# Lambda-layer block, float32, one core: all sixteen output tiles finished by VectorE in two passes

## The chip, the cores and the metric

The kernel runs on one core of a Trainium2 chip. The metric is the time of one execution on the device, in microseconds (us). The time before is the median of three runs.

## The reference: what is computed

The input x has 32 images of 512 channels and 64 x 64 pixels, float32. Per image, cut to what matters:

```python
xn = group_norm(x, 32 groups)                     # mean and variance over 16 channels x 4096 pixels
h = relu(bn1(conv1x1(xn, conv1_w)))               # 512 -> 128 channels
q = bn(conv1x1(h, q_w)); k = softmax(conv1x1(h, k_w)); v = bn(conv1x1(h, v_w))
pos = conv 15x15 of each of the 32 planes of v with 16 filters emb
out = einsum(q, k v^T) + einsum(q, pos)           # content and position parts, 4 heads x 32 = 128 channels
h = relu(bn2(out))
h = bn3(conv1x1(h, conv3_w))                      # 128 -> 512 channels
return x + relu(h + xn)                           # xn is the residual
```

The last line is what the change touches. With r the reciprocal deviation of the group (`rcur`), and b the folded bias less r times the group mean (`bcur`), it is x + relu(conv + r x + b), which equals max(conv + (1 + r) x + b, x).

## The kernel before

One image is worked on after the other, in a loop of 31 passes with a prologue for image 0 and an end for image 31. The order of the work is written out by hand, for each engine apart, and semaphores tie the engines together. One pass has two stages.

The lambda stage (`lam`): TensorE alternates between making the position weights (`w1.0` to `w5.7`, line 510, into the PSUM buffers `ring0` and `ring1`, moved to SBUF by ScalarE or VectorE on line 701) and multiplying them with V (line 655, into `ring2` and `ring3`). The content part (line 609) and a remainder (line 619) stand at its start and middle. VectorE takes the group statistics of the next image there.

The mixed stage (`mixed`, in the order `MIX`): it joins the front of the next image to the output of the present one. The front has four chunks of 1024 pixels: `c0` to `c3` (conv1, line 529), `q0` to `q3` (line 536), `k0` to `k3` (line 541, keys and values), the small products `nb`, `cl`, `cp`. The output has sixteen tiles of 128 channels x 1024 pixels, `o0.0` to `o3.3`; tile `oJ.T` has the number n = 4J + T. The stage ends with the first weights of the next image, `w0.0` to `w0.7`, and the remainders `r0`, `r1` (line 519). The order is

```python
c0 nb c1 q0 k0 o0.0 o0.1 c2 q1 k1 o0.2 o0.3 c3 q2 k2 o1.0 o1.1 q3 k3 o1.2 o1.3 o2.0 o2.1 cl o2.2 cp o2.3
o3.0 w0.0 o3.1 w0.1 o3.2 w0.2 o3.3 w0.3 w0.4 w0.5 w0.6 w0.7 r0 r1
```

TensorE fills one of the four 128 x 1024 PSUM buffers for each name and, before it does, waits until what the buffer held has been taken out (`take`, with the table `moved`). For the end of the stage the buffers are: `cl` follows `o1.2` in one buffer, `o2.2` follows `o1.3`, `cp` follows `o2.0`, `o2.3` follows `o2.1`, `o3.0` follows `o2.3`, `w0.5` follows `w0.3`, `w0.7` follows `w0.5`. `w0.0` waits, too, for the last quarter of the split q, which goes from SBUF to a DRAM buffer and back in another layout (`store_q`, `load_q` on SyncE's queue).

An output tile is finished in one of two ways. For a tile in `VEC_TILES` VectorE makes two passes: line 1022 adds (1 + r) x to the PSUM buffer in place, line 1025 adds the bias, takes the maximum with x and writes into X. For a tile in `POOL_TILES` VectorE makes one pass (line 1018: r x plus the PSUM buffer into an SBUF tile T, which lies in S and is double-buffered), ScalarE applies bias and relu to T (line 740), and GpSimd adds T to X (line 1174). In the second way the PSUM buffer is free after the one VectorE pass (`half_sum`), in the first after both (`out_ready`).

Of the eight weights `w0.s`, VectorE moves `w0.1` and `w0.5`, ScalarE the others. GpSimd also makes the third part of the split q (line 1167, once per chunk) and zeroes borders (line 1160). SyncE issues all transfers in one written order; in it, the outputs 8 to 15 come last, after the loads of V.

Of the kernel before, what the change touches and what calls it, by code (L numbers as in the profile page):

```python
# [43 lines left out]
STATS_AT = {0: (0, 0, 0, 0, 0, 1, 1, 1), 1: (1, 1, 1, 2, 1, 1, 2, 1), 2: (1, 1, 1, 2, 1, 1, 2, 1), 3: (1, 1, 1, 1, 1, 2, 1, 1)}  # L44


VEC_TILES = [1, 4, 7, 10, 13, 15]
POOL_TILES = [n for n in range(16) if n not in VEC_TILES]
NVEC, NPOOL = len(VEC_TILES), len(POOL_TILES)
HEAD = 1  # L50
# [42 lines left out]
def lambda_block(nc, x, w1, bn1, wq, bnq, wk, wv, bnv, emb, bn2, w3, bn3, out):  # L93
# [25 lines left out]
    with ctx:  # L119
# [169 lines left out]
        def moved(name, im):  # L289
# [10 lines left out]
            if name[0] == "o":  # L300
                n = int(name[1]) * CT + int(name[3:])
                if n in POOL_TILES:
                    return [(half_sum, im * NPOOL + HEAD + POOL_TILES.index(n) + 1)]
                return [(out_ready, im * NVEC + HEAD + VEC_TILES.index(n) + 1)]
            if name in ("gm", "gv", "nb", "r0", "r1", "cl", "cp"):
# [33 lines left out]
        def _(sp):  # L339
# [49 lines left out]
            def store_out(b, n):  # L389
# [3 lines left out]
                else:  # L393
                    sp.wait_ge(out_ready, b * NVEC + HEAD + VEC_TILES.index(n) + 1)
                sp.dma_start(ov[b, :, t, j * CHUNK:(j + 1) * CHUNK], X[:, j, t, :]).then_inc(out_done[j], 16)
# [451 lines left out]
        def _(dve):  # L847
# [157 lines left out]
            def output(chain, name, at, b):  # L1005
# [14 lines left out]
                else:  # L1020
                    i = VEC_TILES.index(n)
                    nc.vector.scalar_tensor_tensor(src[:, :], X[:, j, t, :], r1cur[:, t:t + 1], src[:, :],  # L1022
# [210 lines left out]
```

## Time and profile before

| what | us |
|---|---|
| median of 3 runs | 5392.46 (5383.96 to 5400.19) |
| the profiled execution: its own time | 5397.76 |
| its span | 5396.0 |
| TensorE matmul busy | 4680.3 (87%) |
| VectorE busy | 2873.9 (53%) |
| ScalarE busy | 2431.7 (45%) |
| GpSimd busy | 1047.7 (19%) |
| mean granted clock of TensorE | 0.91 |

The busy shares are means over an image; one image takes some 165 us, so the stages have to be read one by one. The rows below are of one image in the middle, whose mixed stage begins at 2534.64 us, and of the end.

### The profile page before, as it was taken

The page shows a single profiled execution, that of the slowest core. Times are in us where ns is not written, and L with a number is a line of the kernel's source. Part 1 is how long each engine was busy: PE and PEld are TensorE (multiplying, and loading weights), DVE is VectorE, ACT ScalarE, POOL GpSimd, SP SyncE. Part 2 cuts the span into 40 slices and gives each one's busy share as a digit, 9 for nine tenths or more (in the row PEclk, how much of TensorE's full clock was granted, in tenths as well). Part 3 has the DMA queues.
Part 4 walks back from the last instruction along what each step waited for, and adds up shares of the span by engine and source line. Part 5 has one row for each costly group of instructions (what it writes and reads, how often), then busy time and mean ns, then how long its engine had stood idle before and what let it go on. Part 6 is the DMA issues. An engine that isn't in the chain of part 4 may idle for free.

```text
span 5396.0 us, 121678 instructions
## 1 busy us (share of the span) xinstructions
PE 4680.3 (87%) x49366; PEld 2721.4 (50%) x49366; DVE 2873.9 (53%) x4567; ACT 2431.7 (45%) x2944; POOL 1047.7 (19%) x561
## 2 busy tenths in 40 slices
PE   4888899888889888898888988889988899888897
PEld 2554455554455544555544555445554455554454
DVE  4455555555554555555555555555455555555553
ACT  1444445444444444444444444444444444444444
POOL 0012221122211122211222111222112221122222
PEclk8898899988998898998899998899998899998998
DMA  3668766678666677666786666876667766678666
GB/s 99 196 220 267 253 192 224 218 240 273 218 206 226 220 265 258 192 220 217 240 273 196 212 220 230 273 238 187 225 228 253 264 191 221 220 233 274 232 194 214
DMA packets 540245, 1217.09 MB, mean 226 GB/s; under 512 B 54313, under 2 KB 236589, under 8 KB 539821
## 3 DMA queue, kind: packets, MB, share of 16 engines
q1 hardware_dynamic: 539820, 1210.21, 67.8%
q8 instruction: 416, 6.82, 0.5%
q14 instruction: 9, 0.07, 0.0%
HBM read 777.68 MB, written 365.22 MB: 212 GB/s over the span
## 4 chain that ended last, share of the span: by engine, by line
PE 63%; SPq 11%; DMA 8%; issue 7%; DVE 6%; ACT 3%; POOL 1%; ACTq 0%; POOLq 0%; DVEq 0%
PE ring L529 16%; PE ring L510 15%; PE ring L655 12%; PE ring L585 7%; DMA q_parts<-region 6%; SPq L356 5%; PE ring L609 4%; PE ring L536 3%; PE ring L541 2%; SPq L363 2%; ACT region L701 2%; DMA Qt<-q_parts 2%; DVE region L701 2%; PE ring L619 2%; SPq L366 1%
## 5 line engine op out<-in xcount | busy, mean ns | idle before, releaser
L701 ACT COPY region<-ring 126x1024 f32<-126x1024 f32 x1184 | 1162.1, 1015 | 1324.4 <-PE ring L510 1307.0
L585 PE MATMUL ring<-h,w3T 128*128 128x512 f32 x2048 | 1047.9, 653 | 141.9 <-DVE S L1018 119.0
L510 PE MATMUL ring<-Qt,Ep 96*126 96x256 bf16 x5120 | 871.5, 309 | 341.2 <-issue 156.1
L1174 POOL TENSOR_TENSOR X<-X,S 128x1024 f32<-128x1024 f32 x320 | 750.7, 2351 | 1147.3 <-ACT S L740 1147.3
L510 PEld LDWEIGHTS ring<-Qt,Ep 96*126 96x126 bf16 x5120 | 622.3, 152 | 659.0 <-issue 483.6
L529 PE MATMUL ring<-X,w1e 128*128 128x512 f32 x2048 | 906.4, 595 | 28.8 <-DVE w1e L895 28.8
L701 DVE COPY region<-ring 126x1024 f32<-126x1024 f32 x352 | 430.8, 1224 | 915.3 <-PE ring L510 914.7
L655 PE MATMUL ring<-region,V 126*32 126x128 f32 x24576 | 857.4, 283 | 18.0 <-DVE region L701 9.9
L655 PEld LDWEIGHTS ring<-region,V 126*32 126x32 f32 x24576 | 654.6, 113 | 143.5 <-issue 117.9
L585 PEld LDWEIGHTS ring<-h,w3T 128*128 128x128 f32 x2048 | 396.9, 207 | 547.8 <-issue 365.1
L529 PEld LDWEIGHTS ring<-X,w1e 128*128 128x128 f32 x2048 | 384.5, 190 | 495.3 <-issue 492.0
L871 DVE BATCH_NORM_STATS2 st<-X 128x6 f32<-128x512 f32 x1024 | 624.2, 679 | 0.0
L740 ACT ACTIVATE S<-S,bcur 128x1024 f32<-128x1024 f32 x320 | 366.7, 1146 | 538.6 <-DVE S L1018 534.2
L973 DVE SCALAR_TENSOR_TENSOR region<-ring,pbi,region 64x512 f32<-64x512 f32 x256 | 179.4, 739 | 787.6 <-ACT region L790 566.8
L1018 DVE SCALAR_TENSOR_TENSOR S<-X,rcur,ring 128x1024 f32<-128x1024 f32 x320 | 405.6, 1275 | 121.7 <-PE ring L585 119.1
L1167 POOL TENSOR_TENSOR region<-region 64x1024 bf16<-64x1024 f32 x128 | 273.0, 2133 | 936.1 <-ACT region L794 931.2
L1160 POOL MEMSET region<- 64x224 f32 x32 | 13.2, 413 | 2259.1 <-PE ring L655 2215.2
L784 ACT ACTIVATE region<-ring,nb 128x1024 f32<-128x1024 f32 x128 | 142.0, 1109 | 506.4 <-DVE nb L902 299.4
L1022 DVE SCALAR_TENSOR_TENSOR ring<-X,r1cur,ring 128x1024 f32<-128x1024 f32 x192 | 246.7, 1285 | 206.8 <-PE ring L585 202.4
L541 PEld LDWEIGHTS ring<-wkvT,region 128*128 128x128 f32 x2048 | 238.2, 191 | 103.9 <-issue 77.9
L541 PE MATMUL ring<-wkvT,region 128*128 128x48 f32 x2048 | 254.1, 277 | 0.0
L609 PE MATMUL ring<-Qt,CLp 96*32 96x512 bf16 x1024 | 245.8, 1092 | 7.2 <-DMA Qt<-v_rest 7.2
(127 smaller groups left out, 3018.7 us busy)
## 6 DMA issues: line engine op xcount, KB each, us to landing
X<-x_dram SPq DMA_DIRECT2D x256, 2048.0 KB, 11.9
out_dram<-X SPq DMA_DIRECT2D x512, 512.0 KB, 6.6
Qt<-q_parts SPq DMA_DIRECT2D x768, 128.0 KB, 2.8
V<-v_windows SPq DMA_DIRECT2D x96, 1024.0 KB, 10.9
h<-S SPq DMA_DIRECT2D x1024, 64.0 KB, 2.0
q_parts<-region SPq DMA_DIRECT2D x128, 256.0 KB, 4.5
v_windows<-region SPq DMA_DIRECT2D x64, 512.0 KB, 6.1
V<-v_windows SPq DMA_DIRECT2D x32, 672.0 KB
```

What stands on the lines that cost most here:

```text
L510: last = nc.tensor.matmul(dst[0:TROWS, i * 256:(i + 1) * 256], taps(u, xo, yo), Q[:, :, xo * BLK + yo, :], start=(i % 2 == 0), stop=True, ...
L529: last = nc.tensor.matmul(dst[:, hh * HALF:(hh + 1) * HALF], w1e[:, c, :], X[:, j, c, hh * HALF:(hh + 1) * HALF], start=(c == 0), stop=(c ...
L541: last = nc.tensor.matmul(dst[:, i * KV:(i + 1) * KV], h1[:, j % 2, i * P:(i + 1) * P], wkvT[:, :], start=True, stop=True)
L585: last = nc.tensor.matmul(dst[:, yb * HALF:(yb + 1) * HALF], w3T[:, t, :], src, start=True, stop=True)
L609: nc.tensor.matmul(bank_of(k)[c * DV:(c + 1) * DV, :], CLp[:, :], Qg[:, :, c, half * 32:half * 32 + 32, 4 * k:4 * k + 4] .rearrange("p h n ...
L655: last = nc.tensor.matmul(bank_of(i)[c * DV:(c + 1) * DV, (g % 4) * P:(g % 4 + 1) * P], V[0:TROWS, VSLOT[t], xb, yb * DV:(yb + 1) * DV], W ...
L701: return engine_copy(dst, src)
L740: nc.scalar.activation(T[:, i % 2, :], T[:, i % 2, :], ACT.Relu, bias=bcur[:, n % CT:n % CT + 1]).then_inc(half_relu, 1)
L871: return nc.vector.bn_stats(st[:, c, 2 * j + hh, :], X[:, j, c, hh * HALF:(hh + 1) * HALF])
L1018: nc.vector.scalar_tensor_tensor(T[:, i % 2, :], X[:, j, t, :], rcur[:, t:t + 1], src[:, :], ALU.mult, ALU.add).then_inc(half_sum, 1)
L1167: nc.gpsimd.tensor_tensor(q12[:, 1, cols], r1[:, j % 2, :], q12[:, 0, cols], ALU.subtract)\
L1174: nc.gpsimd.tensor_tensor(X[:, j, t, :], X[:, j, t, :], T[:, i % 2, :], ALU.add).then_inc(pool_out, 1)
```

## The change

One line of the tables changes; all sixteen numbers stand in `VEC_TILES` now, and `POOL_TILES` is empty, so that `NVEC` is 16 and `NPOOL` is 0:

```diff
-VEC_TILES = [1, 4, 7, 10, 13, 15]
+VEC_TILES = list(range(16))
 POOL_TILES = [n for n in range(16) if n not in VEC_TILES]
 NVEC, NPOOL = len(VEC_TILES), len(POOL_TILES)
```

What this does to VectorE's instructions at two places follows. The first is the loop's part from `o1.2` to `o2.3` (tiles 6 to 11), with the small products `cl` (L994) and `cp` (L997 to L1003) between them. Before:

```order
L1018 SCALAR_TENSOR_TENSOR S<-X,rcur,ring 128x1024
L1022 SCALAR_TENSOR_TENSOR ring<-X,r1cur,ring 128x1024
L1025 SCALAR_TENSOR_TENSOR X<-ring,bcur,X 128x1024
L1018 SCALAR_TENSOR_TENSOR S<-X,rcur,ring 128x1024
L1018 SCALAR_TENSOR_TENSOR S<-X,rcur,ring 128x1024
L994 COPY Qt<-ring 16x32
L1022 SCALAR_TENSOR_TENSOR ring<-X,r1cur,ring 128x1024
L1025 SCALAR_TENSOR_TENSOR X<-ring,bcur,X 128x1024
...
L1003 CAST CLp<-clt 96x32
L1018 SCALAR_TENSOR_TENSOR S<-X,rcur,ring 128x1024
```

And now:

```order
L1022 SCALAR_TENSOR_TENSOR ring<-X,r1cur,ring 128x1024
L1025 SCALAR_TENSOR_TENSOR X<-ring,bcur,X 128x1024
L1022 SCALAR_TENSOR_TENSOR ring<-X,r1cur,ring 128x1024
L1025 SCALAR_TENSOR_TENSOR X<-ring,bcur,X 128x1024
L1022 SCALAR_TENSOR_TENSOR ring<-X,r1cur,ring 128x1024
L1025 SCALAR_TENSOR_TENSOR X<-ring,bcur,X 128x1024
L1022 SCALAR_TENSOR_TENSOR ring<-X,r1cur,ring 128x1024
L1025 SCALAR_TENSOR_TENSOR X<-ring,bcur,X 128x1024
L994 COPY Qt<-ring 16x32
L1022 SCALAR_TENSOR_TENSOR ring<-X,r1cur,ring 128x1024
...
```

Four tiles ahead of or at `o2.3` (`o1.2`, `o2.0`, `o2.1` and `o2.3` itself) have a second pass that was not there. The second place is the end of the mixed stage on VectorE, from the move of `w0.1` to that of `w0.5` (L701), with the tiles `o3.2` and `o3.3` between them:

```order
 L701 COPY region<-ring 126x256x4
 L1009 REGISTER_ALU
-L1015 REGISTER_ALU
-L1018 SCALAR_TENSOR_TENSOR S<-X,rcur,ring 128x1024
-L1022 SCALAR_TENSOR_TENSOR ring<-X,r1cur,ring 128x1024
-L1024 REGISTER_ALU
+L1022 SCALAR_TENSOR_TENSOR ring<-X,r1cur,ring 128x1024
+L1025 SCALAR_TENSOR_TENSOR X<-ring,bcur,X 128x1024
+L1022 SCALAR_TENSOR_TENSOR ring<-X,r1cur,ring 128x1024
 L1025 SCALAR_TENSOR_TENSOR X<-ring,bcur,X 128x1024
 L910 REGISTER_ALU
 L701 COPY region<-ring 126x256x4
```

The second pass of `o3.2` now stands ahead of the move of `w0.5`. On ScalarE and GpSimd the ten instructions of line 740 and the ten of line 1174 go from each image; GpSimd keeps the four of line 1167. SyncE's transfers and TensorE's matmuls keep their order; ten of the output stores wait for VectorE where they waited for GpSimd.

## Rows read from the trace of the kernel before

**Rows 1.** The page: chain that ended last, shares of the span.

```profile
PE 63%; SPq 11%; DMA 8%; issue 7%; DVE 6%; ACT 3%; POOL 1%; ACTq 0%; POOLq 0%; DVEq 0%
```

**Rows 2.** Windows of one image: busy us (instructions) of each engine, clock, DMA.

```profile
2595.79:2613.10 17.31, 11.47 (x78) 5.94 (x78) 12.78 (x18) 4.59 (x4) 9.36 (x4) 0.77 0.76 201
2613.10:2634.35 21.25, 16.16 (x57) 8.90 (x56) 11.18 (x10) 10.40 (x11) 4.70 (x2) 0.66 1.02 346
```

**Rows 3.** Waits of TensorE: us in total, times, longest us.

```profile
PE ring L585 <- DVE S L1018: 119.0, 31, 3.9
PE ring L510 <- DMA Qt<-q_parts: 108.6, 32, 7.6
```

**Rows 4.** Timeline of TensorE, `cl` to `o3.1`: start us, us, line, [idle before].

```profile
2597.88 3.13 PE L557 MATMUL ring<-region,kS 128*16 128x32 f32 x64 [2.09 <-DVE S L1018]
...
2609.32 3.78 PE L585 MATMUL ring<-h,w3T 128*128 128x512 f32 x4 [3.75 <-DVE S L1018]
2616.20 1.11 PE L510 MATMUL ring<-Qt,Ep 96*126 96x256 bf16 x4 [3.10 <-DMA Qt<-q_parts]
2617.10 3.62 PE L585 MATMUL ring<-h,w3T 128*128 128x512 f32 x4
```

**Rows 5.** TensorE's shortest `o3.0`, in another image.

```profile
4597.22 1.98 PE L585 MATMUL ring<-h,w3T 128*128 128x512 f32 x4 [3.89 <-DVE S L1018]
```

**Rows 6.** VectorE's groups by line: busy us, mean ns of one.

```profile
L1022 DVE SCALAR_TENSOR_TENSOR ring<-X,r1cur,ring 128x1024 f32<-128x1024 f32 x192 | 246.7, 1285 | 206.8 <-PE ring L585 202.4
L1025 DVE SCALAR_TENSOR_TENSOR X<-ring,bcur,X 128x1024 f32<-128x1024 f32 x192 | 246.6, 1284 | 6.8
```

**Rows 7.** Timeline of VectorE, `k3` to `o2.3`, the same image.

```profile
2592.21 1.38 DVE L986 TENSOR_TENSOR kS<-kS,kst 128x128 f32<-128x128 f32 x1
...
2594.06 1.81 DVE L959 TENSOR_TENSOR kS<-kS,kst 128x128 f32<-128x128 f32 x1
...
2596.55 1.28 DVE L1018 SCALAR_TENSOR_TENSOR S<-X,rcur,ring 128x1024 f32<-128x1024 f32 x1
...
2603.41 1.29 DVE L1022 SCALAR_TENSOR_TENSOR ring<-X,r1cur,ring 128x1024 f32<-128x1024 f32 x1 [0.36 <-PE ring L585]
...
2606.43 1.06 DVE L1000 CAST clh<-clt 96x32 bf16<-96x32 f32 x1
```

**Rows 8.** Timeline of GpSimd beside it.

```profile
2591.09 2.35 POOL L1174 TENSOR_TENSOR X<-X,S 128x1024 f32<-128x1024 f32 x1 [5.18 <-ACT S L740]
2593.60 2.12 POOL L1167 TENSOR_TENSOR region<-region 64x1024 bf16<-64x1024 f32 x1 [0.16 <-POOL X L1174]
...
2602.79 4.66 POOL L1174 TENSOR_TENSOR X<-X,S 128x1024 f32<-128x1024 f32 x2 [1.28 <-ACT S L740]
```

**Rows 9.** L1000 over all images: ns min/median/max.

```profile
L1000 DVE CAST clh<-clt x32: 178/1386/1401, 133.0 to 5252.3; 96x32 bf16<-96x32 f32 x32
```

**Rows 10.** Timeline of VectorE, `o3.1` to the move of `w0.5`.

```profile
2620.76 1.29 DVE L1022 SCALAR_TENSOR_TENSOR ring<-X,r1cur,ring 128x1024 f32<-128x1024 f32 x1 [6.25 <-PE ring L585]
...
2624.41 1.27 DVE L1018 SCALAR_TENSOR_TENSOR S<-X,rcur,ring 128x1024 f32<-128x1024 f32 x1
2625.95 1.29 DVE L1022 SCALAR_TENSOR_TENSOR ring<-X,r1cur,ring 128x1024 f32<-128x1024 f32 x1 [0.26 <-PE ring L585]
...
2628.51 1.23 DVE L701 COPY region<-ring 126x1024 f32<-126x1024 f32 x1
```

**Rows 11.** Timeline of the end on VectorE: the first passes and the last.

```profile
5360.34 1.28 DVE L1018 SCALAR_TENSOR_TENSOR S<-X,rcur,ring 128x1024 f32<-128x1024 f32 x1 [16.35 <-PE ring L585]
5362.06 1.29 DVE L1022 SCALAR_TENSOR_TENSOR ring<-X,r1cur,ring 128x1024 f32<-128x1024 f32 x1 [0.43 <-PE ring L585]
...
5364.58 2.46 DVE L1018 SCALAR_TENSOR_TENSOR S<-X,rcur,ring 128x1024 f32<-128x1024 f32 x2
...
5389.18 1.28 DVE L1025 SCALAR_TENSOR_TENSOR X<-ring,bcur,X 128x1024 f32<-128x1024 f32 x1
```

**Rows 12.** Timeline of the end, GpSimd's last.

```profile
5389.20 2.34 POOL L1174 TENSOR_TENSOR X<-X,S 128x1024 f32<-128x1024 f32 x1 [1.23 <-ACT S L740]
```

## Prediction

> **What bounds the kernel now.** I read the chain that ended last first. TensorE holds 63% of it, and VectorE only 6% [rows 1], so VectorE's added work counts only where TensorE waits for it. The waits of TensorE say where that is: 119.0 us in 31 waits of an output tile for a VectorE pass of line 1018, and 108.6 us in 32 waits of a weight for the split q to come back from DRAM [rows 3]. The timeline of one image puts both in the last third of the mixed stage [rows 4]: `cl` waits 2.09 us for the pass of `o1.2`; `o3.0` waits 3.75 us, at 2609.32, for the pass of `o2.3`, which held its PSUM buffer; and `w0.0`, two rows on, waits 3.10 us, at 2616.20, for q. The windows agree: between 2595.79 and 2613.10 VectorE is busy 12.78 of 17.31 us and TensorE 11.47, at a mean granted clock of 0.77, and in the next 21.25 us the clock is 0.66 [rows 2]. Of the ten tiles that get a second pass, those before `o1.1` are finished long before anything needs VectorE again (it is idle for most of the first part of the stage, up to `q2`), so I count them at nothing; they would cost 1.3 us each if that idle time were gone. Everything is decided between `k3` and the move of `w0.5`.
>
> **The price of a pass.** Lines 1022 and 1025 take 1.285 and 1.284 us by the profile [rows 6]; one pair takes 2.52 us from start to start (5362.06 to 5364.58), and two passes of line 1018 take 2.46 us together, so some 1.2 us each from start to start [rows 11]. A tile that changes sides costs VectorE 1.3 us more. The same pair of instructions runs 192 times already, so this price is read, not bounded.
>
> **Step 1: up to `o2.3`.** VectorE gets to `q3` 1.3 us later, by the second pass of `o1.1`. That is not handed on. Before, line 986 of `k3` took 1.38 us beside GpSimd's add of 2591.09, and line 959 took 1.81 us and ended as GpSimd's split (line 1167, 2593.60 for 2.12 us) ended [rows 7, 8]. Without the add, line 986 should be short, and it makes up the 1.1 us; line 959 still ends with the split, at about 2595.8, since the split itself starts no sooner: its input is 1.3 us later, and the add it had to wait for is gone. So `o1.2` starts at 2596.55 as before. From there the second passes of `o1.2`, `o2.0`, `o2.1` and `o2.3` add 4 x 1.3 = 5.2 us. Two things come off: the 0.36 us of idle time before `o2.2` [rows 7], and the stall of line 1000, 1.06 us here beside GpSimd's adds of 2602.79 [rows 7, 8], against a shortest of 0.18 us over all images [rows 9]: 0.88 us. `o2.3` is out of its buffer 5.2 - 0.36 - 0.88 = 4.0 us later, and `o3.0` starts 4.0 us later.
>
> The page SBUF — State Buffer of the Trainium skill (SBUF: two separate sides) says that VectorE and GpSimd share one pair of ports, as an exclusive lock that the first one holds for its whole instruction; the rows of lines 959, 986 and 1000 agree with it. By that rule alone the change would save VectorE all those stalls: line 986's 1.1 us as well as line 1000's, and the sum below would be 1.1 us per image, 34 us in all, lower. I don't count it, since line 959 has the split beside it in any case.
>
> **Step 2: what covers it.** `w0.0` did not start when `o3.0` ended but a mean of (108.6 - 7.6) / 31 = 3.26 us later, when q was back [rows 3] (the longest wait, 7.6 us, is the prologue's). q's way is issued by SyncE and doesn't wait for VectorE's output tiles of this part, and ten stores become ready earlier, not later, so q is back no later than before. The wait is therefore eaten first: `w0.0` starts 4.0 - 3.26 = 0.74 us later, if `o3.0` takes as long as before. The 2.09 us wait before `cl` grows by 1.3 us, and a new wait of some 2 us appears before `cp` and `o2.3` (the copy of `cl` on VectorE stands behind `o2.1`), but both lie ahead of `o3.0` and inside its 4.0 us.
>
> **Step 3: from `o3.1` to `w0.5`.** Behind `o3.1`, VectorE runs without a pause except one of 0.26 us, until the move of `w0.5` at 2628.51 [rows 10], and `w0.7`, the remainders and the next image's first weights hang on that buffer. The second pass of `o3.2` adds 1.3 - 0.26 = 1.04 us. That of `o3.0` fits in the 6.25 us idle before `o3.1` [rows 10], and costs nothing while TensorE takes 3 us for a tile. ScalarE's relu of `o3.2` goes, but the weights that ScalarE moves there are not the last to be waited for any more. The output stores 8 to 15 come behind the loads of V in SyncE's order, and the last one is issued after VectorE has it, also when that is 2 us later.
>
> **Step 4: TensorE's clock.** This is the part that no row of before settles. `o3.0` took 3.78 us in this image, at the lower level (1.2 GHz), behind a wait; in another image it took 1.98 us, at 2.4 GHz, behind a wait just as long [rows 4, 5]. Over the 31 images I read from 1.98 to 3.78 us, with a mean of 3.1. `o3.1`, behind the second wait, took 3.62 us here and in most images. With the change the wait for q is gone, so `o3.0`, `w0.0` and `o3.1` run without a pause, but more waiting lies ahead of `o3.0`. Bounds: `o3.0` from 1.1 us less to 0.65 us more than its mean; `o3.1` from 1.7 us less (1.9 instead of 3.6) to nothing. I leave `o3.0` as it is and take half of the bound for `o3.1`, -0.9 us, since it would be the third piece of work in a row.
>
> **Sum.** Per image 0.74 + 1.04 - 0.9 = +0.9 us, by 31 passes of the loop: +28 us. After the loop, all sixteen tiles stand alone. VectorE starts them at 5360.34 and the last add on GpSimd ended at 5389.20 + 2.34 = 5391.54 [rows 11, 12]. Sixteen pairs take 16 x 2.52 = 40.3 us, so the last tile is ready at 5400.7, 9 us later, with TensorE ahead of VectorE by then (1.9 us for a tile against 2.5); the last store behind it costs the same as now, some 4.4 us. Together +37 us on the profiled execution's 5397.8, which gives 5435. That execution is 5.3 us above the median of the runs shown, so I state 5392.5 + 37 = 5430 us.
>
> **The rivals.**
> The clock stays low to the end of the stage. For it: the longer waits before `cl`, `o2.3` and `o3.0`, each of which was followed by 3 to 4 us at the lower level where it can be seen. Then `o3.0` takes 3.78 us in all images and `o3.1` keeps its 3.62: 0.74 + 1.04 + 0.65 = +2.4 us per image, 75 + 9 = +84 us, 5477.
> The cover is all but enough. If `o3.1` gets the full 1.7 us back, or the stalls beside GpSimd all go as the exclusive lock would allow (1.1 us per image more than I count), the per-image cost falls to -0.2 to +0.1 us, and what is left is the end: +3 to +12 us, about 5400. Against it: the split still runs beside `k3`.
> Faster. If the clock stays at 2.4 GHz through both `o3.0` (-1.1) and `o3.1` (-1.7), the image is 0.74 + 1.04 - 2.8 = -1.0 us: -32 + 9 = -23 us, 5370. It decides from -0.3 us per image on, where the loop pays for the end. One image shows 1.98 us behind a 3.9 us wait [rows 5], most don't, and the clock would have to hold through three waits.
> VectorE saturated elsewhere. If `q3` or `k3` were delayed by the full 1.3 us (line 986 caught behind the split), each image costs 1.3 us more: +40 us, 5470. The rows of before show line 986 at 1.38 us only beside the add.
>
> **How the numbers follow.** No change can be told from a change of about 0.3% here (16 us). The forecast (+0.4 to +1.6 us per image, its own range 5413 to 5451) gets 0.45; the low clock 0.17; the delayed `k3` 0.07; the cover that is enough 0.22; faster 0.09. The range goes from the cover case to the low clock, 5388 to 5477; it leaves out the faster case and a little above. Slower by over 0.3% (above 5409) is the forecast and both dear cases, less a margin: 0.65; within 0.3% 0.26; faster 0.09.
>
> **What the changed profile would show.** Lines 740, 1018 and 1174 gone; lines 1022 and 1025 512 times each at 1.28 us; VectorE busy 10 x 32 x 1.28 = 410 us more, less some 70 us of stalls. Line 1000 at 0.18 us, line 986 at 0.29 throughout, line 959 long still. `o3.0` waiting for line 1025 some 4 us later in the image, and no wait of `w0.0` for q. `w0.7` waiting over 1 us for line 701 on VectorE. The last pass ending at about 40.3 us from the first. The prediction is wrong if TensorE still waits for q (then step 2's price is too high), or if `o3.0` and `o3.1` are both near 1.9 us or both near 3.7 (then step 4 decides, either way).

## The result and the profile after

The changed kernel takes 5430.65 us (median of 4 runs, 5426.77 to 5437.91) beside 5390.03 us for the kernel before: a ratio of 1.0075, with a 95% interval of 1.0055 to 1.0095. It is slower, by 0.75%. The profiled execution has a span of 5435.9 us where the one before had 5396.0: +39.9 us.

First the page of the changed kernel: busy time of each engine, and the chain that ended last by engine.

```profile
PE 4693.3 (86%) x49366; PEld 2718.5 (50%) x49366; DVE 3200.2 (59%) x4887; ACT 2077.6 (38%) x2624; POOL 294.2 (5%) x241
...
PE 66%; DVE 18%; issue 11%; ACT 2%; SPq 1%; DMA 1%; DVEq 0%; ACTq 0%; POOL 0%
```

VectorE is busy 3200.2 us, 326 more than before; GpSimd lost 754 us and ScalarE 354. VectorE's share of the chain went from 6% to 18%, DMA's from 8% to 1% and that of SyncE's issues (SPq) from 11% to 1% [rows 1]: TensorE now waits for VectorE where it waited for q. The groups of VectorE show the price of a pass unchanged [rows 6], 512 times each:

```profile
L1022 DVE SCALAR_TENSOR_TENSOR ring<-X,r1cur,ring 128x1024 f32<-128x1024 f32 x512 | 656.1, 1281 | 143.3 <-PE ring L585 142.3
...
L1025 DVE SCALAR_TENSOR_TENSOR X<-ring,bcur,X 128x1024 f32<-128x1024 f32 x512 | 657.5, 1284 | 18.2
```

The waits of TensorE (us in total, times, longest) stand beside [rows 3]. The wait for q is gone, and a wait of `cp` (line 561) for VectorE's copy of `cl` has come up: 86.8 us in 32 waits. That of the output tiles (line 585) for VectorE is about as long as before in total, on line 1025 instead of 1018.

```profile
PE ring L585 <- DVE X L1025: 117.8, 84, 3.9
PE ring L561 <- DVE Qt L994: 86.8, 32, 3.4
PE ring L557 <- DVE X L1025: 84.6, 31, 2.7
```

The timeline of TensorE in one image of the changed kernel, whose c0 starts at 2547.65 us, answers to [rows 4]: `cl`, `cp`, `o3.0`, `w0.0`, `o3.1`, `w0.7`.

```profile
2612.12 2.04 PE L557 MATMUL ring<-region,kS 128*16 128x32 f32 x64 [2.73 <-DVE X L1025]
...
2619.98 0.34 PE L561 MATMUL ring<-Qt 16*96 16x32 f32 x2 [3.35 <-DVE Qt L994]
...
2626.15 3.78 PE L585 MATMUL ring<-h,w3T 128*128 128x512 f32 x4 [3.11 <-DVE X L1025]
2629.72 1.06 PE L510 MATMUL ring<-Qt,Ep 96*126 96x256 bf16 x4
2630.58 2.35 PE L585 MATMUL ring<-h,w3T 128*128 128x512 f32 x4
...
2642.93 1.11 PE L510 MATMUL ring<-Qt,Ep 96*126 96x256 bf16 x4 [2.20 <-DVE region L701]
```

`o3.0` starts 78.5 us after c0 where it started 74.7 us after it. `w0.0` follows `o3.0` without a wait, at 82.1 instead of 81.6. `o3.1` takes 2.35 us instead of 3.62, and `w0.7` now waits 2.20 us for the move of `w0.5` on VectorE. The windows of the same two stretches (up to the end of `o3.0`, and from there to the next image's first weights) show where VectorE's time went and what TensorE's clock did, to be read against [rows 2]:

```profile
2609.39:2629.93 20.54, 10.87 (x80) 5.18 (x80) 16.29 (x19) 0.00 (x0) 0.00 (x0) 0.79 0.90 256
2629.93:2647.50 17.57, 13.98 (x57) 7.71 (x56) 13.63 (x12) 8.33 (x9) 0.00 (x0) 0.79 1.06 381
```

The second stretch has a mean clock of 0.79 where it had 0.66, and is 17.6 us long instead of 21.3. VectorE in the same image, from `k3` to the move of `w0.5`, with GpSimd's split beside `k3` as the first line, beside [rows 7, 8, 10]:

```profile
2606.51 2.13 POOL L1167 TENSOR_TENSOR region<-region 64x1024 bf16<-64x1024 f32 x1 [7.77 <-ACT region L794]
...
2606.36 0.29 DVE L986 TENSOR_TENSOR kS<-kS,kst 128x128 f32<-128x128 f32 x1
...
2607.12 1.67 DVE L959 TENSOR_TENSOR kS<-kS,kst 128x128 f32<-128x128 f32 x1
...
2609.46 1.28 DVE L1022 SCALAR_TENSOR_TENSOR ring<-X,r1cur,ring 128x1024 f32<-128x1024 f32 x1
...
2622.89 0.18 DVE L1000 CAST clh<-clt 96x32 bf16<-96x32 f32 x1
...
2624.81 1.28 DVE L1025 SCALAR_TENSOR_TENSOR X<-ring,bcur,X 128x1024 f32<-128x1024 f32 x1
...
2632.97 1.29 DVE L1022 SCALAR_TENSOR_TENSOR ring<-X,r1cur,ring 128x1024 f32<-128x1024 f32 x1 [0.40 <-PE ring L585]
...
2639.14 1.28 DVE L1022 SCALAR_TENSOR_TENSOR ring<-X,r1cur,ring 128x1024 f32<-128x1024 f32 x1
...
2641.66 1.21 DVE L701 COPY region<-ring 126x1024 f32<-126x1024 f32 x1
```

Line 986 takes 0.29 us and line 1000 0.18: the stalls beside GpSimd's adds are gone. Line 959 still takes 1.67 us and ends as the split ends (2608.79 and 2608.64). The passes of `o1.2` to `o2.3` now run from 2609.46 to 2626.09.

The table has the means over the 30 inner images of the loop, read from the timelines of TensorE and SyncE of one profiled execution of each kernel. All times are in us after c0 of the image, except the duration of `o3.1`; the load of q counts as issued when SyncE is through with it.

| | `cl` | `cp` | `o3.0` | q's last load issued | `w0.0` | `o3.1` takes | `r0` | next c0 |
|---|---|---|---|---|---|---|---|---|
| before | 63.24 | 68.59 | 74.69 | 78.66 | 81.05 | 3.54 | 95.43 | 165.18 |
| changed | 64.47 | 72.32 | 78.69 | 75.21 | 82.06 | 2.14 | 95.93 | 166.07 |
| early tiles only | 63.14 | 68.45 | 74.58 | 75.05 | 77.87 | 2.42 | 91.06 | 161.34 |
| late tiles only | 64.56 | 72.42 | 78.71 | 78.70 | 82.22 | 2.27 | 96.37 | 166.35 |
| `o0.0` only | 63.24 | 68.60 | 74.68 | 76.21 | 78.67 | 2.71 | 92.16 | 162.58 |
| queue order only | 63.23 | 68.61 | 74.68 | 76.70 | 79.07 | 3.06 | 92.85 | 162.88 |
| all but `o3.2` | 64.47 | 72.32 | 78.70 | 75.04 | 82.04 | 2.25 | 95.22 | 165.96 |
| all but tiles 6, 8, 9, 11 | 63.23 | 68.37 | 74.58 | 75.20 | 78.07 | 2.54 | 92.34 | 161.93 |
| changed, idle matmuls | 64.47 | 72.25 | 78.50 | 75.25 | 80.90 | 1.93 | 94.54 | 165.38 |
| changed, T in SBUF | 63.14 | 72.30 | 77.73 | 74.72 | 80.04 | 1.97 | 93.75 | 163.85 |

The first two rows of the table hold a surprise: q's last load is issued 3.45 us earlier in the changed kernel. The experiments are about that as much as about the loss.

How fine can the table be read? Two pairs of profiles can tell. The changed kernel and the kernel of experiment 6 have the same loop, and their images take 166.07 and 165.77 us; the early tiles alone were profiled twice, with 161.34 and 161.62. Up to `r0` the first pair agrees to 0.12 us and the second to 0.42; from `r0` to the next c0 they differ by 0.42 and 0.70. So differences below some 0.4 us in the last column say nothing.

### The profile page after: what moved, and what is told of

The parts are those of the page before. It is cut to its first block, busy times and chain, and to the rows that moved or that the text cites. A ratio compares the mean times of both kernels' runs of the same rounds, so it can differ in the third digit from the quotient of the medians.

```text
span 5435.9 us, 120080 instructions
## 1 busy us (share of the span) xinstructions
PE 4693.3 (86%) x49366; PEld 2718.5 (50%) x49366; DVE 3200.2 (59%) x4887; ACT 2077.6 (38%) x2624; POOL 294.2 (5%) x241
## 4 chain that ended last, share of the span: by engine, by line
PE 66%; DVE 18%; issue 11%; ACT 2%; SPq 1%; DMA 1%; DVEq 0%; ACTq 0%; POOL 0%
PE ring L529 16%; PE ring L510 14%; PE ring L655 12%; PE ring L585 10%; DVE ring L1022 8%; PE ring L609 4%; PE ring L536 3%; DVE X L1025 3%; PE ring L541 2%; DVE region L701 2%; PE ring L619 2%; ACT region L701 1%; DVE region L973 1%; ACT region L790 1%; DVE Qt L705 1%
## 5 line engine op out<-in xcount | busy, mean ns | idle before, releaser
L701 ACT COPY region<-ring 126x1024 f32<-126x1024 f32 x1184 | 1161.7, 1016 | 1936.8 <-PE ring L510 1920.4
L585 PE MATMUL ring<-h,w3T 128*128 128x512 f32 x2048 | 1065.2, 659 | 135.0 <-DVE X L1025 117.8
L510 PE MATMUL ring<-Qt,Ep 96*126 96x256 bf16 x5120 | 858.7, 306 | 278.4 <-issue 150.9
L701 DVE COPY region<-ring 126x1024 f32<-126x1024 f32 x352 | 430.3, 1223 | 924.6 <-PE ring L510 924.6
L655 PE MATMUL ring<-region,V 126*32 126x128 f32 x24576 | 864.2, 285 | 17.6 <-DVE region L701 9.9
L1022 DVE SCALAR_TENSOR_TENSOR ring<-X,r1cur,ring 128x1024 f32<-128x1024 f32 x512 | 656.1, 1281 | 143.3 <-PE ring L585 142.3
L1025 DVE SCALAR_TENSOR_TENSOR X<-ring,bcur,X 128x1024 f32<-128x1024 f32 x512 | 657.5, 1284 | 18.2
L536 PE MATMUL ring<-region,wqT 128*64 128x512 f32 x512 | 247.1, 605 | 0.0
L794 ACT CAST region<-region 64x1024 bf16<-64x1024 f32 x128 | 133.4, 1042 | 277.4 <-DVE region L973 277.4
L790 ACT ACTIVATE region<-ring,pbi 64x512 bf16<-64x512 f32 x256 | 160.6, 676 | 133.4 <-PE ring L536 133.4
```

The lines of the kernel that those rows point to most:

```text
L510: last = nc.tensor.matmul(dst[0:TROWS, i * 256:(i + 1) * 256], taps(u, xo, yo), Q[:, :, xo * BLK + yo, :], start=(i % 2 == 0), stop=True, ...
L536: last = nc.tensor.matmul(dst[0:QC, hh * HALF:(hh + 1) * HALF], wqT[:, :], h1[:, j % 2, hh * HALF:(hh + 1) * HALF], start=True, stop=True)
L585: last = nc.tensor.matmul(dst[:, yb * HALF:(yb + 1) * HALF], w3T[:, t, :], src, start=True, stop=True)
L655: last = nc.tensor.matmul(bank_of(i)[c * DV:(c + 1) * DV, (g % 4) * P:(g % 4 + 1) * P], V[0:TROWS, VSLOT[t], xb, yb * DV:(yb + 1) * DV], W ...
L701: return engine_copy(dst, src)
L1025: nc.vector.scalar_tensor_tensor(X[:, j, t, :], src[:, :], bcur[:, t:t + 1], X[:, j, t, :], ALU.add, ALU.max).then_inc(out_ready, 1)
```

## The experiments

Each is compared with runs of the kernel before on the same chip. Their medians there were 5403 to 5406 us, so only the ratios are compared.

**1. The early tiles alone.** Tiles 0, 2, 3 and 5, which stand ahead of `q3`, go to VectorE; the six later ones stay.

```diff
-VEC_TILES = list(range(16))
+VEC_TILES = [0, 1, 2, 3, 4, 5, 7, 10, 13, 15]
```

> Only the four tiles that stand ahead of q3 (o0.0, o0.2, o0.3, o1.1) go to VectorE in two passes, on top of the six of before; the six later ones (o1.2, o2.0, o2.1, o2.3, o3.0, o3.2) stay with ScalarE and GpSimd. My theory, as in the prediction: these four cost nothing in the loop and nothing else moves, o3.0 and w0.0 start where they did, image 165.2 us; the end has four more second passes on VectorE (10 x 2.52 + 6 x 1.2 = 32.4 us, hardly longer than the 31 us of before): 5390 to 5396 us. Rival: since the stores of these tiles are ready earlier, SyncE's queue gets to q's transfers sooner (in the changed kernel q is back some 78 us after c0, in the kernel before 81), and w0.0, which waits for q there, starts up to 3 us earlier: 162 us per image, 5300 us. Second rival: they are the ones that delay k3: 1.3 us per image, 5430 us.

Measured: 5286.66 us, ratio 0.9797 (0.9769 to 0.9824). The first rival holds, and the gain is a little larger than its 5300 us: `w0.0` comes 3.2 us sooner, `o3.1` takes 2.42 us instead of 3.54, and the image takes 161.3 us. The theory carried over from the prediction, that these four tiles cost nothing and move nothing else, fails in its second half. The timeline of TensorE shows `cl`, `o3.0`, `w0.0` and `o3.1` in an image whose c0 is at 2489.04:

```profile
2552.18 2.04 PE L557 MATMUL ring<-region,kS 128*16 128x32 f32 x64 [1.40 <-DVE S L1018]
...
2563.63 3.78 PE L585 MATMUL ring<-h,w3T 128*128 128x512 f32 x4 [3.88 <-DVE S L1018]
2567.20 1.06 PE L510 MATMUL ring<-Qt,Ep 96*126 96x256 bf16 x4
2568.05 2.44 PE L585 MATMUL ring<-h,w3T 128*128 128x512 f32 x4
```

`o3.0` waits for line 1018 as before and starts at 74.6 after c0, as before, but `w0.0` (2567.20) now has q there as soon as TensorE is free. In 25 of 30 images it doesn't wait for a transfer at all.

**2. The late tiles alone.** The complement.

```diff
-VEC_TILES = list(range(16))
+VEC_TILES = [1, 4, 6, 7, 8, 9, 10, 11, 12, 13, 14, 15]
```

> The complement: the six later tiles in two passes, o0.0, o0.2, o0.3 and o1.1 by ScalarE and GpSimd as before. My theory: all of the loop's loss comes with these six, +0.9 us per image; line 986 beside the add of o1.1 stays stalled; the end is 12 x 2.52 + 4 x 1.2 = 35.0 us on VectorE against 31, +4: 5390 + 28 + 4 = 5422 us. Rival (early tiles share in the loss, or in a gain by earlier stores): under 5405, or over 5435.

Measured: 5440.81 us, ratio 1.0072 (1.0046 to 1.0099). The late six by themselves cost what the whole change costs (1.0075), although the early four by themselves gain 2%. The two don't add up, since `w0.0` waits for the later of two things: for q, whose last load is issued at 78.7 here and at 75.2 in the changed kernel, and for `o3.0`, which ends near 82 in both.

The two runs also tell apart what GpSimd's adds did to VectorE. Line 986 (of `k3`, beside the add of `o1.1`, an early tile) and line 1000 (beside the adds of `o2.0` and `o2.1`, late tiles), durations in ns as min/median/max; first the early tiles on VectorE, line 986 and then line 1000:

```profile
L986 DVE TENSOR_TENSOR kS<-kS,kst x128: 291/291/294, 99.4 to 5125.6; 128x128 f32<-128x128 f32 x128
```

```profile
L1000 DVE CAST clh<-clt x32: 177/1379/1394, 133.5 to 5138.3; 96x32 bf16<-96x32 f32 x32
```

And the late tiles on VectorE, the same two lines:

```profile
L986 DVE TENSOR_TENSOR kS<-kS,kst x128: 291/291/1395, 99.0 to 5275.8; 128x128 f32<-128x128 f32 x128
```

```profile
L1000 DVE CAST clh<-clt x32: 176/177/178, 133.0 to 5293.5; 96x32 bf16<-96x32 f32 x32
```

Each stall goes with its add and stays without it. The page SBUF — State Buffer of the Trainium skill (SBUF: two separate sides) describes an exclusive lock of the ports that VectorE and GpSimd share; the runs agree. Line 1025, one of whose inputs is in PSUM, took 1.28 us beside the adds and without them: in the kernel before, 103 of its 192 runs overlap an add.

**3. The first tile alone, and the queue's order alone.** These ask why the early tiles bring q sooner. In the kernel before, SyncE's order is: store q's first quarter, store `o0.0`, load q's first quarter, store `o0.1`, reload x's third chunk, and so on. SyncE in the kernel before (c0 at 2534.64): the store of `o0.0`, the load of q's first quarter, and the reload of x's fourth chunk.

```profile
2563.63 0.38 SPq L395 DMA_DIRECT2D out_dram<-X  x1
2564.14 3.80 SPq L356 DMA_DIRECT2D Qt<-q_parts  x6
...
2584.86 0.41 SPq L344 DMA_DIRECT2D X<-x_dram  x1
```

And in the changed kernel (c0 at 2547.65):

```profile
2571.86 1.82 SPq L395 DMA_DIRECT2D out_dram<-X  x1
2575.14 3.79 SPq L356 DMA_DIRECT2D Qt<-q_parts  x6
...
2594.87 0.41 SPq L344 DMA_DIRECT2D X<-x_dram  x1
```

The store of `o0.0` stood in the queue until GpSimd was through with it, 29.0 us after c0; now it goes at 24.2. What follows it is sooner by 2 us for the load of q (29.5 against 27.5) and by 3 us for the reload, 50.2 against 47.2. The first experiment gives only this tile to VectorE:

```diff
-VEC_TILES = [1, 4, 7, 10, 13, 15]
+VEC_TILES = [0, 1, 4, 7, 10, 13, 15]
```

> Only the first tile (o0.0) goes to VectorE in two passes, on top of the six of before. The theory that the runs so far leave (A): its store stands in SyncE's order ahead of the load of q's first quarter, and waited for GpSimd until about 29 us after c0; with the store ready at 24 the reloads of x that follow in the queue are issued 3 us sooner and get out of the way of q's next stores, so q's last quarter is back 3 us sooner. Then this one tile gives most of what the four early ones gave: 162 us per image, about 5310 us. Rival B: the load on GpSimd, ScalarE or VectorE's shared port is what mattered, one tile of four gives about a quarter of it: 164.2 us per image, 5370. Rival C: the last early tile (o1.1), whose store stands right ahead of q3's store, is the one: no gain here, 5400.

Measured: 5320.1 us, ratio 0.9843 (0.9818 to 0.9868), 162.6 us per image. One tile of the four gives three quarters of their gain; rivals B and C, at 5370 and 5400 us, fall. The second leaves all tiles of the kernel before as they are and swaps two entries of SyncE's order:

```diff
                 store_q(b + 1, 0)
-                store_out(b, 0)
                 load_q(b + 1, 0)
+                store_out(b, 0)
```

> The kernel before, with all tiles divided as before; in SyncE's order alone, the store of o0.0 and the load of q's first quarter change places. Theory A (a store in SyncE's order holds up the transfers behind it): most of the gain of the early tiles appears without any change of the compute engines: 162 to 163 us per image, 5310 to 5340 us. Rival B (the engines' load): no gain, 5400.

Measured: 5334.61 us, ratio 0.9865 (0.9843 to 0.9886), 162.9 us per image. SyncE there, with c0 at 2506.66: the load of q's first quarter at 27.5, two stores behind it, and the reload of the fourth chunk at 49.4.

```profile
2534.13 3.79 SPq L356 DMA_DIRECT2D Qt<-q_parts  x6
2538.11 1.09 SPq L395 DMA_DIRECT2D out_dram<-X  x2
...
2556.09 0.41 SPq L344 DMA_DIRECT2D X<-x_dram  x1
```

Theory A holds: 1.35% of the 2.03% that the early tiles gain comes without touching a compute engine, from a store that no longer holds up the transfers behind it. Why an earlier reload brings q's last quarter sooner can be read from the landing times in the traces, though it wasn't tried by itself. Means over the 30 images, in us after c0:

| | reload of chunk 4 issued | it has landed | store of q's third quarter issued | it has landed | q's last load has landed |
|---|---|---|---|---|---|
| before | 50.3 | 59.8 | 51.4 | 60.8 | 80.8 |
| queue order only | 48.9 | 58.1 | 51.3 | 59.1 | 78.8 |
| `o0.0` only | 48.7 | 57.7 | 51.3 | 58.8 | 78.4 |
| early tiles only | 47.0 | 56.6 | 51.1 | 57.6 | 77.2 |

The store of q's third quarter is issued at nearly the same time in all four kernels, but it lands about 1 us behind the reload that was issued just ahead of it. The load of this quarter waits for that, SyncE waits with the load, and q's last quarter comes behind. Read this way, q's own transfers were held up twice: by a store that waited for GpSimd, and by a reload of x that had been issued late for that reason.

**4. One tile given back: `o3.2`.**

```diff
-VEC_TILES = list(range(16))
+VEC_TILES = [n for n in range(16) if n != 14]
```

> The changed kernel, with o3.2 (tile 14) alone given back to ScalarE and GpSimd. Step 3 of the prediction puts 1.04 us per image on its second pass, ahead of the move of w0.5: the remainders start 1.0 us sooner after c0 (94.9 instead of 95.9), the image is 1.0 us shorter, the end some 1 us shorter: 5400 to 5405 where the changed kernel gives 5435. Rival: the pass is covered, since o3.1 got faster, no change.

Measured: 5420.61 us (10 runs), ratio 1.0021 (1.0009 to 1.0033), against the changed kernel's 1.0075: 0.54%, or 29 us, less, near the 33 expected (1.04 us by 31 images and 1 at the end). The profile, which is of the slowest of its runs (5404.29 to 5435.9), shows the pass itself: from the end of `o3.1` to `r0` it is 10.14 us where the changed kernel has 10.99 and the kernel before 9.98. `r0` comes 0.71 us sooner, and that the next c0 is only 0.1 us sooner is within what two profiles of one loop differ by.

**5. Four tiles given back: `o1.2`, `o2.0`, `o2.1`, `o2.3`.**

```diff
-VEC_TILES = list(range(16))
+VEC_TILES = [0, 1, 2, 3, 4, 5, 7, 10, 12, 13, 14, 15]
```

> The changed kernel with the four tiles between k3 and o3.0 (o1.2, o2.0, o2.1, o2.3) given back to ScalarE and GpSimd; o3.0 and o3.2 stay on VectorE. Step 1 of the prediction: o3.0 starts 4 us sooner, 74.7 us after c0. As q is back early in this division, w0.0 follows at 77.9 as with the early tiles alone, and the one cost left is the 1.04 us of o3.2: 161.3 + 1.0 = 162.4 us per image, about 5325 us. Rival: the costs don't add up this way, since the second pass of o3.0 costs too: above 5340.

Measured: 5307.77 us, ratio 0.9817 (0.9797 to 0.9837), 161.9 us per image. `o3.0` is back at 74.58 and `w0.0` at 78.07. Against the early tiles alone, `r0` is later by 1.3 us (92.34, 91.06), of which 0.96 lies behind `o3.1`, where the second pass of `o3.2` is; a cost of the second pass of `o3.0`, the rival's, doesn't show. So the four tiles ahead of `o3.0` are worth 1.0075 - 0.9817 = 2.6%, by far the most of what the late tiles cost once q is early.

**6. The end.** The loop as changed, the last image divided as before.

```diff
+END_VEC = [1, 4, 7, 10, 13, 15]
+END_POOL = [n for n in range(16) if n not in END_VEC]
...
-            for n in POOL_TILES:
+            for n in END_POOL:
                 relu_half(B - 1, n)
...
-            for n in POOL_TILES:
+            for n in END_POOL:
                 add_x(B - 1, n)
```

> The changed kernel in the loop, but the last image's sixteen tiles are divided as before (six by VectorE, ten through ScalarE and GpSimd). My theory: the end gives back what the longer chain of VectorE costs, 9 to 10 us: 5421 us, image still 166.1 us. Rival: the end is bound by the output stores and not by VectorE, no difference to the changed kernel, 5430.

Measured: 5431.33 us (8 runs, 5418.39 to 5455.76), ratio 1.0066 (1.0046 to 1.0086): beside 1.0075 that is inconclusive, the 10 us looked for are no more than the intervals. The profiles are clearer: from the last c0 to the end of the span it is 215.5 us before, 226.0 changed, and 215.9 here. Some 3 us of this are no part of the end, since the first pass over the sixteen tiles starts 182.6 us after the last c0 in the changed kernel and at 179.6 here, behind the same code. From that pass to the end of the span it is 35.7 us before, 43.5 changed and 36.3 here, so the divided end is worth 7.2 us. The last image's passes in the changed kernel, the first, the third and the last of 32, beside [rows 11, 12]:

```profile
5392.42 1.29 DVE L1022 SCALAR_TENSOR_TENSOR ring<-X,r1cur,ring 128x1024 f32<-128x1024 f32 x1 [16.66 <-PE ring L585]
...
5394.94 1.28 DVE L1022 SCALAR_TENSOR_TENSOR ring<-X,r1cur,ring 128x1024 f32<-128x1024 f32 x1
...
5431.49 1.28 DVE L1025 SCALAR_TENSOR_TENSOR X<-ring,bcur,X 128x1024 f32<-128x1024 f32 x1
```

They run without a pause from 5392.42 to 5432.77, 40.35 us.

**7. TensorE kept busy while it waits.** Matmuls whose results nobody reads stand before `cp` (16 of them) and before `o3.0` (20).

```diff
+            def fill(dst, n):
+                for _ in range(n):
+                    nc.tensor.matmul(dst[0:TROWS, 0:256], Ep[:, 0, 0:TROWS], Ep[:, 1, 0:256],
+                                     start=True, stop=True, skip_group_check=True)
...
+                if name == "o3.0" and at is AT_MIX:
+                    fill(ring[3], FILL[name])
```

> The changed kernel with idle matmuls added on TensorE (bf16, 126 x 256, constant operands, results never read): 16 before cp and 20 before o3.0, in buffers that are free there, so that TensorE is busy while it waits for VectorE. My theory: the 3.5 us that o3.0 takes are the lower clock level; kept busy, TensorE does it in 2.0 us, w0.0 follows 1.5 us sooner, and each image is 1.0 to 1.5 us shorter: 5385 to 5400. Rival (the length of o3.0 has another cause, its operands or the DMA traffic): o3.0 stays at 3.5 us, 5430 or a little more.

Measured: 5410.29 us (10 runs), ratio 1.0011 (0.9993 to 1.0029), 0.64% less than the changed kernel, an image of 165.4 us. The timeline shows the 20 idle matmuls, `o3.0`, `w0.0` and `o3.1`:

```profile
2623.36 2.37 PE L591 MATMUL ring<-Ep 96*126 96x256 bf16 x20
2627.51 1.98 PE L586 MATMUL ring<-h,w3T 128*128 128x512 f32 x4 [1.78 <-DVE X L1035]
2629.33 0.60 PE L511 MATMUL ring<-Qt,Ep 96*126 96x256 bf16 x4
2629.77 1.88 PE L586 MATMUL ring<-h,w3T 128*128 128x512 f32 x4
```

`o3.0` takes 1.98 us and `o3.1` 1.88, with the same operands as ever, at a granted clock of 1.00 in both; in the kernel before, the clock is 0.50 during the 3.78 and the 3.62 us of [rows 4]. So these are the lower level of the clock, 1.2 GHz, after a wait, and not the data. Over all images `o3.0` has a mean of 2.59 us here and 3.57 in the changed kernel. Of the 1.4 us that `r0` gained, 0.7 was left at the next c0.

**8. The same with the early tiles alone**, first with 20 short matmuls before `o3.0`, then with 5 longer ones.

```diff
-VEC_TILES = list(range(16))
+VEC_TILES = [0, 1, 2, 3, 4, 5, 7, 10, 13, 15]
...
+FILL = {"cp": 0, "o3.0": 20}
```

> The four early tiles on VectorE as in the run before of that division, and 20 idle matmuls (bf16, 126 x 256, constant operands) before o3.0, so that TensorE is busy while it waits for VectorE. There w0.0 followed o3.0 (3.3 us at the lower clock) in most images, with q back at about the same time. Theory (the clock of o3.0 and o3.1 is the next bound): o3.0 in 2.0 us, w0.0 some 0.5 us sooner where q allows, o3.1 in 1.9 instead of 2.4 us: 0.5 to 1 us per image, 5260 to 5275 us where the early tiles alone gave 5287. Rival (q's way through DRAM is the next bound): w0.0 waits for q instead, under 0.3 us per image, 5280 to 5290 us.

Measured: 5375.72 us, ratio 0.9938 (0.9917 to 0.996). Both theories fall. `r0` is sooner, at 90.1 after c0 instead of 91.1, as the first one says, and yet the image takes 164.7 us and not 161.3. TensorE's waits show where the 3 us went, to idle time that this view puts down to nothing ("issue"):

```profile
PE ring L511 <- issue: 268.5, 89, 6.1
...
PE ring L511 <- DMA Qt<-q_parts: 37.6, 29, 7.9
```

> The early tiles on VectorE, and the idle matmuls before o3.0 in another shape: 5 of float32, 128 x 512, in place of 20 of bf16, 126 x 256. With the 20, TensorE's idle time in which it waits for nothing that the profile shows grew from 144 to 269 us on line 510, right behind the loop's start. Theory: that time hangs on the number of instructions in the loop; with 5 it is near 144 us again, and the image gains the 0.5 to 1 us at r0 that the 20 gave there (90.1 instead of 91.1 us after c0): 5260 to 5275 us. Rival: it hangs on TensorE arriving earlier at the loop's start while transfers hold the memory, whatever the number: again over 200 us, 5340 to 5380 us.

> The division with the four early tiles on VectorE once more, on the chip of the filler run, for a comparison beside it: ratio to the kernel before 0.977 to 0.983, idle time of TensorE without a shown cause on line 510 near 144 us.

Measured: 5384.28 us, ratio 0.9968 (0.9948 to 0.9987) with the five long ones; 5281.43 us, ratio 0.9766 (0.9749 to 0.9782), for the early tiles again, which bears out experiment 1 on another chip. In the latter:

```profile
PE ring L510 <- issue: 150.6, 62, 5.0
```

With the five it is 293.8 us in 90 waits. So it isn't the mere number of added instructions. The added time lies at the loop's start: from `r0` to the content part it is 8.1 us with the 20 and 8.9 with the 5, and 4.4 with the early tiles alone (means over 30 images).

The traces say more than the waits do. One of the transfer queues, which the profile calls "instruction", brings blocks of 16 KB. Its packets with the early tiles alone, with the 20 matmuls, and with the 5:

```profile
q8 instruction: 415, 6.80, 0.5%
```

```profile
q8 instruction: 446, 7.31, 0.6%
```

```profile
q8 instruction: 444, 7.27, 0.6%
```

That is 31 and 29 blocks more for the 31 passes of the loop. And with the 20, in the image whose `r0` starts at 2794.91, TensorE stands still ahead of the content part (line 619 there):

```profile
2794.91 2.08 PE L520 MATMUL ring<-Qt,E 96*22 96x256 bf16 x8
2802.50 1.96 PE L511 MATMUL ring<-Qt,Ep 96*126 96x256 bf16 x8 [5.51 <-issue]
```

A block is on its way from 2799.86 on, and TensorE goes on 1.7 us after it has landed. In all fourteen profiles, each of TensorE's idle times of over 2 us that are put down to "issue" behind the first c0 ends 1.2 to 1.8 us after such a block has landed. The kernels without idle matmuls have one such idle time per image, of some 3.8 us; with the 20 and with the 5, 26 and 30 of them stand ahead of the content part, 117 and 149 us in all, where the early tiles alone have one. That is the added time. It looks as if TensorE ran out of instructions there, for one more block per pass; this is read from coinciding times and no run was made to test it. The extra block alone isn't enough: experiment 7 has 446 too, but its `r0` is 4 us later and only 8 images wait ahead of the content part. Why the block comes so late behind the early tiles stays open.

**9. The buffer or the engine.** Two passes as in the changed kernel, but the first writes into the SBUF tile T, so that the PSUM buffer is free after one.

```diff
-                return [(out_ready, im * NVEC + HEAD + VEC_TILES.index(n) + 1)]
+                return [(whole_sum, im * NVEC + VEC_TILES.index(n) + 1)]
...
-                    nc.vector.scalar_tensor_tensor(src[:, :], X[:, j, t, :], r1cur[:, t:t + 1], src[:, :],
+                    nc.vector.scalar_tensor_tensor(T[:, i % 2, :], X[:, j, t, :], r1cur[:, t:t + 1], src[:, :],
...
-                    nc.vector.scalar_tensor_tensor(X[:, j, t, :], src[:, :], bcur[:, t:t + 1], X[:, j, t, :],
+                    nc.vector.scalar_tensor_tensor(X[:, j, t, :], T[:, i % 2, :], bcur[:, t:t + 1], X[:, j, t, :],
```

> The changed kernel, two VectorE passes for all sixteen tiles, but the first pass writes to the SBUF tile T (two buffers) in place of the PSUM buffer, which is thus free after one pass; the number of passes is the same. It tells VectorE's time from the time that a PSUM buffer is held. Theory: three of the 4.0 us by which o3.0 is late are VectorE's time (three second passes ahead of o2.3), 1.3 us are the holding of o2.3's own buffer. cl starts at 63.2 us after c0 instead of 64.5, o3.0 at 77.4 instead of 78.7, w0.0 at 80.8; the image is about 1.3 us shorter, 5390 to 5400 us where the changed kernel gives 5435. Rival 1 (the holding of buffers is all of it): o3.0 back at 74.7, 5320. Rival 2 (the second pass, with two SBUF inputs, is slower or is held up beside GpSimd's splits): no gain, 5435 or more.

Measured: 5371.63 us, ratio 0.9939 (0.9917 to 0.9961), so 1.4% less than the changed kernel and less than the kernel before. `cl`, `cp`, `o3.0` and `w0.0`, with c0 at 2514.29:

```profile
2577.42 2.04 PE L557 MATMUL ring<-region,kS 128*16 128x32 f32 x64 [1.62 <-DVE S L1024]
...
2586.59 0.52 PE L561 MATMUL ring<-Qt 16*96 16x32 f32 x2 [4.66 <-DVE Qt L994]
...
2592.19 1.98 PE L585 MATMUL ring<-h,w3T 128*128 128x512 f32 x4 [1.37 <-DVE S L1024]
2594.01 0.60 PE L510 MATMUL ring<-Qt,Ep 96*126 96x256 bf16 x4
```

`cl` is back at 63.1 after c0; `cp` is where it was, since the copy of `cl` on VectorE is behind `o2.1` in both; `o3.0` starts at 77.7 (means of the table), 1.0 us sooner and not 1.3. So three quarters of the 4 us are VectorE's time and one quarter is the held buffer. The rest of the gain was not expected. TensorE waits 1.37 us before `o3.0` in every image here, where the changed kernel waits a mean of 3.11, and the granted clock during `o3.0` has a mean of 0.86 instead of 0.54, so that `o3.0` to `w0.0` takes a mean of 2.31 us instead of 3.37. Rival 2 came true for one pass per image: beside the first split, 22.1 us after c0, the second pass (both inputs in SBUF now) takes 1.78 us instead of 1.28, and TensorE doesn't wait for it there.

## Why the prediction was right, and where it wasn't

The forecast was 5430 us; 5430.65 was measured. The direction and the size are right, and the agreement to under 1 us is luck: the interval of the ratio alone allows 30 to 51 us of loss beside the 37 forecast, and the median of before moved from 5392.46 to 5390.03 with a fourth run. The sum was +0.9 us per image and +9 at the end. The two profiles show +0.89 and +10.5, and 2.8 us more in the first image. That, too, is less exact than it looks. By the pieces, in us per image:

| | forecast | measured |
|---|---|---|
| up to `w0.0` (steps 1 and 2) | +0.74 | +1.01 |
| `w0.0` and `o3.1`, the clock (step 4) | -0.9 | -1.53 |
| end of `o3.1` to `r0` (step 3) | +1.04 | +1.01 |
| `r0` to the next c0 | nothing | +0.39 |

The last piece is within what two profiles of one loop differ by (0.42 and 0.70 us there). The 2.8 us of the first image say little either: the profile of the kernel before has 148.5 us for it, and every other profile 149.9 to 153.6, also that of the kernel in which only SyncE's order differs (151.2). Up to `r0`, where the steps can be followed, the loss is 0.50 us and not 0.88. By its own steps:

- **Step 1, up to `o2.3`: right.** +4.0 us for `o3.0` was worked out, 74.69 to 78.69 measured. The second pass of `o1.1` cost nothing beyond `k3`: line 986 fell from 1.38 to 0.29 us and line 959 ended with the split. Line 1000 fell to 0.18 us. That the full saving under the exclusive lock doesn't arrive, because the split holds line 959 anyway, was right too. The run with T in SBUF adds that a quarter of the 4 us is the holding of `o2.3`'s buffer.
- **The early tiles "at nothing", and q at its old time in step 2: wrong, and it changed nothing in the sum.** The prediction wrote that q "is back no later than before", which is true, and then counted with q at the same time as before. It took "ten stores become ready earlier" as harmless and stopped there. The first of them unblocked SyncE's queue, and q's last load was issued 3.45 us sooner. The early tiles by themselves gain 2.0% by it (experiment 1), and 1.35% comes by the queue's order alone (experiment 3). In the sum it made no difference, since step 2's other half was right: with `o3.0` 4 us late, `w0.0` no longer waits for q at all, however soon it comes. The late tiles cost 1.0075 - 0.9797 = 2.8% against the early tiles alone, not the 0.75% that the comparison with the kernel before shows. The cover that step 2 counted, 3.26 us of waiting, came for the most part from the queue's order and not from the work.
- **Step 3: right.** 1.04 us for the second pass of `o3.2`: from the end of `o3.1` to `r0` it is +1.01 us, and 0.85 of it goes again in experiment 4, whose median is 29 us lower.
- **Step 4: the direction is right, both sizes are off.** `o3.0` takes 3.57 us instead of 3.11, +0.46 where nothing was counted, and is at the lower level of the clock nearly throughout. `o3.1` takes 2.14 instead of 3.54, -1.40 where -0.9 was chosen as half of a bound. The two errors partly cancel.
- **The end: right for VectorE, 1.3 us too much for the whole.** 16 x 2.52 = 40.3 us worked out, 40.35 measured, 9.15 more than the 31.2 of before. The last store ends 1.3 us sooner behind its tile, so the end costs 7.8 us. The other 2.75 us up to +10.5 are the tiles' later start after the last c0 (182.56 against 179.81 us); experiment 6, with the same code ahead of them, starts them at 179.60, so this is no cost of the change.

Of the rivals, the low clock came for `o3.0` (3.57 us, near the rival's 3.78) and not for `o3.1`, and the delayed `k3` didn't come. "The cover is all but enough" wanted 1.7 us from `o3.1` and got 1.40, with `o3.0` longer besides. No rival had the early tiles in it, and the largest effect in this change was there.

## What to carry to other kernels

When a store moves to an earlier time, look at what stands behind it in its queue: a queue that issues in a written order turns one late producer into a delay of all that follows, and here two entries of the order were worth 1.35%. Look at the landing times too: transfers issued late hold up those behind them, as the reload did with q's third quarter. Two effects that end in one wait don't add up, and one of them can be hidden whole: a change that ends at +0.75% held a gain of 2.0%. An engine's added pass is priced at the place where it is waited for, not by its share of busy time: four passes in front of `o3.0` were most of the loss (2.6 of 2.8%), and four others, for which nothing waited, cost nothing that could be seen.

The fastest version is the division of experiment 1, at 0.977 to 0.980 of the kernel before. Whether the swap in SyncE's order adds anything to it was not run.

## What the runs showed that was not expected

Keeping TensorE busy with idle matmuls did raise the clock (`o3.0` in 1.98 us instead of up to 3.78) but made a good kernel slower: 0.9938 and 0.9968 instead of 0.9797 and 0.9766. TensorE's idle time under "issue" on the line of the weights grew from 150.6 us to 268.5 and 293.8, and nearly all of the growth lies right behind the loop's start, in idle times that end just after a 16 KB block of the "instruction" queue has landed. The gain ahead of that place was taken back there, and more. So it pays to look at that queue when TensorE stands idle and no engine is named, and to count its packets in both kernels (415 and 446 here) when instructions are added to a loop.
